# All generated adapter rows in SBUF: the first batch's rows go straight to its weight tile, the stores to DRAM follow the last chunk

## The reference

```python
dWd = ((h_lang @ Wdd.T + bdd) * DELTA_SCALE).reshape(B, BN, D)   # B 16, BN 128, D 256, h_lang 16x64
dWu = ((h_lang @ Wdu.T + bdu) * DELTA_SCALE).reshape(B, D, BN)   # Wdd, Wdu: 32768 x 64 each
Wd_b = Wd + dWd
Wu_b = Wu + dWu
down = relu(einsum('bld,bnd->bln', x, Wd_b) + bd)
up = einsum('bln,bdn->bld', down, Wu_b) + bu
x = x + up
```

## Time and profile before

| | us |
|---|---|
| median of 3 runs | 892.39 (890.39 to 892.61) |
| profiled execution, its own time | 892.63 |
| its span | 890.8 |
| PE busy | 812.6 (91%) |
| DVE busy | 551.5 (62%) |
| ACT busy | 520.9 (58%) |
| POOL busy | 234.1 (26%) |

### The profile page before, as it was taken

How to read it: one execution, slowest core, us unless ns; L and a number is a source line. 1 busy time by engine, 2 the same in 40 slices (tenths; PEclk the granted TensorE clock), 3 DMA queues, 4 the chain that set the end, 5 groups by cost and what they waited for, 6 DMA issues and landing times.

```text
span 890.8 us, 15973 instructions
## 1 busy us (share of the span) xinstructions
PE 812.6 (91%) x5852; PEld 628.5 (71%) x5852; DVE 551.5 (62%) x1063; ACT 520.9 (58%) x808; POOL 234.1 (26%) x333
## 2 busy tenths in 40 slices
PE   6752577999999999999999999999999999999976
PEld 4101446777787878787878787878787787877665
DVE  1213667686767767585858585858585767656424
ACT  1101443566676758585867667666667676765642
POOL 1002213050505142423223241505050505030310
PEclk9755677999999999999999999999999999999999
DMA  9998733334242342525241514333333333320000
GB/s 344 358 416 314 240 139 103 126 99 163 66 166 75 112 134 85 160 86 160 84 162 56 180 58 150 95 121 125 103 130 115 108 120 107 103 101 2 31 13 13
DMA packets 58477, 118.48 MB, mean 133 GB/s; under 512 B 6336, under 2 KB 15936, under 8 KB 55696
## 3 DMA queue, kind: packets, MB, share of 16 engines
q1 hardware_dynamic: 58400, 117.48, 38.8%
HBM read 82.77 MB, written 34.16 MB: 131 GB/s over the span
## 4 chain that ended last, share of the span: by engine, by line
PE 80%; issue 6%; DMA 5%; DVE 4%; POOL 3%; ACT 1%; SPq 1%; POOLq 0%; DVEq 0%; ACTq 0%
PE bank L502 31%; PE bank L708 13%; PE pair_s L663 6%; PE pair_t L502 5%; PE bank L674 3%; PE bank L755 3%; DMA hyp<-in_hyper 3%; PE pair_s L651 3%; PE pair_s L629 3%; PE bank L567 2%; PE pair_t L651 2%; PE bank L573 2%; PE bank L747 2%; PE pair_t L629 1%; PE pair_t L511 1%
## 5 line engine op out<-in xcount | busy, mean ns | idle before, releaser
L708 PE MATMUL bank<-wf,G 128*128 128x256 f32 x512 | 126.6, 391 | 0.7 <-ACT G L884 0.5
L502 PE MATMUL bank<-wup_hi,hD_hi 128*128 128x512 f32 x256 | 110.3, 431 | 4.1 <-POOL hD_lo L1334 3.2
L869 ACT ACTIVATE Pr<-pair_s 128x1024 f32<-128x1024 f32 x64 | 65.6, 1025 | 74.9 <-PE pair_s L651 74.9
L1362 POOL TENSOR_TENSOR x<-x,xcr 128x512 f32<-128x512 f32 x16 | 20.8, 1302 | 335.4 <-DVE x L1197 335.4
L708 PEld LDWEIGHTS bank<-wf,G 128*128 128x128 f32 x512 | 92.2, 189 | 21.9 <-issue 5.8
L502 PE MATMUL bank<-wup_hi,hD_lo 128*128 128x512 f32 x256 | 101.6, 397 | 0.0
L502 PE MATMUL bank<-wup_lo,hD_hi 128*128 128x512 f32 x256 | 101.6, 397 | 0.0
L1139 DVE TENSOR_REDUCE nmax<-pair_s 128x4 f32<-128x1024 f32 x64 | 78.0, 1218 | 20.3 <-PE pair_s L629 20.1
L1163 DVE STREAM_TRANSPOSE oq<-pair_s 128x512 f32<-128x512 f32 x32 | 22.9, 717 | 88.7 <-PE pair_s L663 88.7
L1139 DVE TENSOR_REDUCE nmax<-pair_t 128x4 f32<-128x1024 f32 x64 | 77.5, 1211 | 0.0
L913 ACT ACTIVATE gl<-bank,rsD 128x512 f32<-128x512 f32 x64 | 43.8, 685 | 53.0 <-PE bank L502 52.9
(11 more groups left out here) (183 smaller groups left out, 1995.5 us busy)
## 6 DMA issues: line engine op xcount, KB each, us to landing
hyp<-in_hyper SPq DMA_DIRECT2D x16, 1024.0 KB, 10.2
Qp<-qk_scratch SPq DMA_DIRECT2D x64, 256.0 KB, 5.0
Kp<-qk_scratch SPq DMA_DIRECT2D x64, 256.0 KB, 4.6
qk_scratch<-q_hi SPq DMA_DIRECT2D x16, 512.0 KB, 2.8
qk_scratch<-k_hi SPq DMA_DIRECT2D x16, 512.0 KB, 3.3
tC<-rows_scratch SPq DMA_DIRECT2D x16, 384.0 KB, 4.3
cur_scratch<-gen SPq DMA_DIRECT2D x16, 256.0 KB, 10.1
xT_t<-in_xT SPq DMA_DIRECT2D x16, 256.0 KB, 4.1
```

The costliest lines, as they stand in the source:

```text
L502: mm = pe.matmul(dst, l, r, start=first and i == 0, stop=last and i == 2)
L708: mm = pe.matmul(bank[5][:, r * D:(r + 1) * D], G[:, k, r * P:(r + 1) * P], wf2[:, k, :], start=k == 0, stop=k == FT - 1)
L869: act.activation(Pr[:, p % 4, :, :].rearrange("p a n -> p (a n)"), pair[p % 2][:, :, :].rearrange("p a n -> p (a n)"), ACT.Exp, scale=DH * ...
```

## The change

The tile `gen` becomes 32 KB per partition with a place for each of the 16 chunks, laid over the later weights `wup_hi` and `wup_lo`; `row_t` and `tb`, which lay there, move to the staging area. With a place for each chunk, ACT and DVE no longer wait for a store before they evict, and ACT, DVE and POOL no longer wait for all the stores before turn 0. The loops over chunks are unrolled. The generator weights are laid out in another order, so that one chunk yields eight whole rows of `cur` for each batch. For each chunk SP issues `first_rows(c)`, a copy of batch 0's eight rows from `gen` to `cur` inside SBUF (8 rows of 2 KB). The stores to `cur_scratch` are four DMAs of 1024 KB behind `wqkv_raw`. `wup_raw` waits for them, since it overwrites `gen`. The gather of `cur` for the later batches is one DMA of 128 rows of 2 KB.

```diff
-        gen = staged("gen", [P, 4, HALF], F32, 4 * HALF)
+        row_t = staged("row_t", [NB, 8 * D], F32, 8 * D)
+        tb = staged("tb", [NB, 8, D], F32, 8 * D)
...
+        gen = nc.alloc_sbuf_tensor_at("gen", [P, NCH, HALF], F32, offset=wup_hi_at)
...
-            def generated(i, s):
-
-                sp.wait_ge(gen_act if s % 2 == 0 else gen_dve, i * 2 + (s // 2 + 1))
-                sp.dma_start(cur_scratch[bass.ds(i * 4 + s, 1)].rearrange("o p n -> (o p) n"), gen[:, s, :]).then_inc(gen_out[s], 16)
-
-            with sp.Fori(0, NCH // 4 - 1) as i:
-                for s in range(4):
-
-                    sp.wait_ge(hyp_mm, i * 4 + (s + 1))
-                    sp.dma_start(hyp[:, s, :], hyper[:, bass.ds((i + 1) * (4 * CHC) + s * CHC, CHC)]).then_inc(hyp_in[s], 16)
-                    generated(i, s)
+            def first_rows(c):
+
+                sp.wait_ge(gen_act if c % 2 == 0 else gen_dve, c // 2 + 1)
+                sp.dma_start(cur[8 * c:8 * c + 8, :], gen[0:P:NB, c, :]).then_inc(first_in, 16)
+
+            for c in range(4, NCH):
+                sp.wait_ge(hyp_mm, c - 3)
+                sp.dma_start(hyp[:, c % 4, :], hyper[:, c * CHC:(c + 1) * CHC]).then_inc(hyp_in[c % 4], 16)
+                first_rows(c - 4)
...
             def load_weights(b):
 
-                for u in range(2):
-                    sp.dma_start(cur[64 * u:64 * u + 64, :].rearrange("p (s n) -> p s n", s=2),
-                                 cur_rows[:, :, bass.ds(b, 1), u * D:(u + 1) * D].rearrange("r s o n -> (r o) s n")).then_inc(cur_in, 16)
-                sp.dma_start(tA[:, :, :].rearrange("p a b -> p (a b)"),
-                             rows_scratch[bass.ds(b, 1), 0:2, :].rearrange("o a b -> o (a b)").to_broadcast([P, 2 * D])).then_inc(tA_in, 16)
+                sp.dma_start(cur[:, :], cur_rows[:, bass.ds(b, 1), :].rearrange("r o n -> (r o) n")).then_inc(cur_in, 16)
+                load_gates(b)
 
             load_rows(0)
-            for s in range(4):
-                generated(NCH // 4 - 1, s)
+            for c in range(NCH - 4, NCH):
+                first_rows(c)
             sp.wait_ge(rows_out, 16)
-            for s in range(4):
-                sp.wait_ge(gen_out[s], 16 * (NCH // 4))
-            load_weights(0)
+            load_gates(0)
             sp.dma_start(wqkv_raw[:, :], w_qkv).then_inc(wqkv_in, 16)
 
+            for i in range(4):
+                sp.dma_start(cur_scratch[4 * i:4 * i + 4].rearrange("c p n -> p c n"), gen[:, 4 * i:4 * i + 4, :]).then_inc(gen_out, 16)
...
             sp.dma_start(wf1_raw[:, :], w_f1).then_inc(wf1_in, 16)
+            sp.wait_ge(gen_out, 64)
             sp.dma_start(wup_raw[:, :], w_up).then_inc(wup_in, 16)
...
             def combine(b):
 
-                dve.wait_ge(cur_in, 32 * b + 32)
+                if b == 0:
+                    dve.wait_ge(first_in, 16 * NCH)
+                else:
+                    dve.wait_ge(cur_in, 16 * b)
```

More of the change, by code:

```diff
@@ L307, in cond_seq_kernel @@
         hyp_in = [sem(f"hyp_in{i}") for i in range(4)]
-        gen_out = [sem(f"gen_out{i}") for i in range(4)]
+        gen_out, first_in = sem("gen_out"), sem("first_in")
         hyp_mm, gen_act, gen_dve = sem("hyp_mm"), sem("gen_act"), sem("gen_dve")
@@ L503, in three, with generate @@
                 return mm
-            def generate(i, s):
-                pe.wait_ge(hyp_in[s], i * 16 + 16)
-                if not isinstance(i, int):
-                    pe.wait_ge(gen_act if s % 2 == 0 else gen_dve, i * 2 + (s // 2 - 1))
+            def generate(c):
+                s = c % 4
+                pe.wait_ge(hyp_in[s], c // 4 * 16 + 16)
+                if c >= 4:
+                    pe.wait_ge(gen_act if s % 2 == 0 else gen_dve, c // 2 - 1)
                 for q in range(QTS):
@@ L525, in _ @@
             mm.then_inc(pre_pe, 1)
-            generate(0, 1)
+            generate(1)
             pe.wait_ge(wc_in, 16)
@@ L546, in _ @@
             mm.then_inc(pre_pe, 1)
-            generate(0, 3)
-            with pe.Fori(1, NCH // 4) as i:
-                for s in range(4):
-                    generate(i, s)
+            generate(3)
+            for c in range(4, NCH):
+                generate(c)
             pe.wait_ge(prep, len(PREP))
@@ L776, in _, with generated @@
         def _(act):
-            def generated(i, s):
-                if not isinstance(i, int):
-                    act.wait_ge(gen_out[s], i * 16)
-                act.wait_ge(hyp_mm, i * 4 + (s + 1))
-                act.activation(gen[:, s, :], bank[s][:, :], ACT.Copy).then_inc(gen_act, 1)
+            def generated(c):
+                act.wait_ge(hyp_mm, c + 1)
+                act.activation(gen[:, c, :], bank[c % 4][:, :], ACT.Copy).then_inc(gen_act, 1)
             act.wait_ge(prep, PREP.index("z1") + 1)
             act.activation(zb[:, 1], zb[:, 0], ACT.Exp, scale=-1.0).then_inc(pre_act, 1)
-            generated(0, 0)
+            generated(0)
             act.wait_ge(prep, PREP.index("z2") + 1)
             act.activation(zb[:, 3], zb[:, 2], ACT.Exp, scale=-1.0).then_inc(pre_act, 1)
-            generated(0, 2)
+            generated(2)
             act.wait_ge(prep, PREP.index("tbl") + 1)
@@ L796, in high_part @@
                 act.activation(hi[:, :, :].rearrange("p k n -> p (k n)"), raw[:, :], ACT.Copy).then_inc(act_w, 1)
-            with act.Fori(1, NCH // 4) as i:
-                for s in (0, 2):
-                    generated(i, s)
+            for c in range(4, NCH, 2):
+                generated(c)
             act.wait_ge(rows_out, 16)
             act.wait_ge(prep, len(PREP))
-            for s in range(4):
-                act.wait_ge(gen_out[s], 16 * (NCH // 4))
             def qkv_weights():
@@ L975, in after_last, with generated @@
                 dve.wait_ge(prep, done[0])
-            def generated(i, s):
-                if not isinstance(i, int):
-                    dve.wait_ge(gen_out[s], i * 16)
-                dve.wait_ge(hyp_mm, i * 4 + (s + 1))
-                dve.tensor_copy(gen[:, s, :], bank[s][:, :]).then_inc(gen_dve, 1)
+            def generated(c):
+                dve.wait_ge(hyp_mm, c + 1)
+                dve.tensor_copy(gen[:, c, :], bank[c % 4][:, :]).then_inc(gen_dve, 1)
             mm4 = bank[4][:, 0:KT * NB].rearrange("p (k n) -> p k n", k=KT)
@@ L1031, in _ @@
             assert done[0] == len(PREP)
-            with dve.Fori(1, NCH // 4) as i:
-                for s in (1, 3):
-                    generated(i, s)
+            for c in range(5, NCH, 2):
+                generated(c)
             def low_part(hi, lo, raw, step_):
@@ L1047, in _ @@
             dve.wait_ge(rows_out, 16)
-            for s in range(4):
-                dve.wait_ge(gen_out[s], 16 * (NCH // 4))
             def combine(b):
-                dve.wait_ge(cur_in, 32 * b + 32)
+                if b == 0:
+                    dve.wait_ge(first_in, 16 * NCH)
+                else:
+                    dve.wait_ge(cur_in, 16 * b)
                 dve.wait_ge(dve_w, at(DVE_W, "base", 0))
@@ L1292, in _ @@
             pool.wait_ge(rows_out, 16)
-            for s in range(4):
-                pool.wait_ge(gen_out[s], 16 * (NCH // 4))
             pool.wait_ge(zero, 7)
@@ L1436 @@
         "x": c(x.reshape(NB, RT, P, D).transpose(0, 2, 1, 3)),
[L1437 to L1439 removed]
+        "hyper": c(np.concatenate([by_part(arr(L0_cond_Wdd).T), arr(L0_cond_Wdu).T.reshape(HC, D, BN).transpose(0, 2, 1)], 2)
+                   .reshape(HC, P // 2, 2, 2 * D).transpose(2, 0, 1, 3).reshape(2 * HC, -1)),
         "base": c(np.concatenate([by_part(wd)[0], wu.T, by_part(bdd)[0], bdu.T], 1)),
```

19 lines of the change are left out of this document (8 added, 11 removed).

## The result

| | median of 14 runs, us | profiled span |
|---|---|---|
| before | 891.42 (889.59 to 892.61) | 890.8 |
| changed | 894.53 (892.71 to 897.61) | 892.6 |

The ratio over all runs is 1.0047, with a 95% interval of 1.0036 to 1.0057; the two medians alone stand 3.1 us or 0.35% apart. 889.9 was forecast (884.5 to 893.8), and the measured time lies outside the range. The head start is there, and more than all of it is gone before the second turn.

The account below looks back on a forecast made before the run. It took the front as bound by the 16 DMA engines and PE as full from the eighth slice on. 5.5 (generation) + 5.8 (tail) - 8.8 (turn 0 waiting) = 2.5 us gained: 889.9, range 884.5 to 893.8.

Parts of the forecast that it names:

- head start: Start of turn 0: `combine(0)` at 61.2 us instead of 72.52, so turn 0 starts 11.3 us earlier.
- The deciding row: DVE's second `cur<-cur,base_c`: expected near 93 us after waiting 16 us or more; at 96 the kernel is no faster.
- The ledger of the queue: DMA queue before batch 1's loads: `wqkv_raw` at 66.0 to 66.4 us, 10.4 of stores, everything behind 0 to 0.6 later.
- the other branch: PE in turn 0: `a_down(1)` starts with `xT_t` at 94.3 us, and DVE's `x` gains 2.8 us.
- the forecast landing: Batch 1's gather of `cur`: within a few tenths of its present landing, with 93.1 us taken for DVE.
- the forecast gain: Whole kernel: DVE's first maximum of turn 1 starts 2.5 us earlier, and this is carried to the end.
- The generation term: Chunk loop: 2.47 us a chunk without stores among the loads, so chunk 15 lands 5.5 us earlier, at 56.0.
- The tail's 5.8: Behind the last chunk: one 16 KB copy, taken as 2.3 us, replaces store and gather; 5.8 us saved.
- The third term, -8.8: Turn 0 waiting for the queue that now holds the stores: 8.8 us lost.
- the queue's idle gap: DMA queue from behind the last store (67.6 us) to the gather's issue: claimed to be moved by the change, not filled.
- the debt that outweighs the head start: Rival at DVE's `A.cur` of batch 1: kernel slower, 893.5 to 897 us; chance 0.12.
- the three conditions: For a slower kernel: reads below 386 GB/s, stores over 12.5 us, or the queue running dry during SP's wait.

## Why the prediction was wrong

**What it had right.** PE's full middle: what happens at the front arrives at the end as a shift. The deciding row, DVE's second `cur`. The ledger of the queue: it had 37.1 us from the last matmul's start (56.0) to `combine(1)` (93.1); measured are 95.45 - 57.79 = 37.7. The wait on `gen_out` without effect of its own (402, 392 and 430 GB/s in the three steps of 2 us from 76), SP reaching the gather ahead of the time of before, the lower level of the clock in `a_down(1)`.

**The step that failed.** "On the other branch `a_down(1)` starts with `xT_t` at 94.3 instead of 98.99". It doesn't: PE runs in program order, and `a_v` stands in front of it with the line `pe.wait_ge(dve_a, at(DVE_A, "qlo1", a))`, since v is accumulated in the bank from which `q_lo` reads. So the branch was not another one but the same chain: gather, `combine(1)`, `q_lo`, v, `Va`, `a_down`, `a_up`. The prediction had PE done with v "before 88" by shifting the whole of PE's turn by 11.3 us, without asking for each row which engine it waits for, although it had just found that `q_lo` would not shift. It thus had 1.2 us from `combine(1)` to `a_down(1)` (93.1 to 94.3) where 5.24 were measured (95.45 to 100.69): 0.6 to `q_lo`, 0.9 to v, 2.97 to `Va`, 0.7 to `a_down`. From `a_down(1)` to `x` it had 4.7, the lower level of the clock counted in, and 4.73 were measured. So of the 6.4 us by which `x` is later than forecast (105.42 against 99.0), 4.0 are the links of the chain that it left out, and 2.4 the later landing. 1.4 of the 4.0 are the lower level of the clock in v, which it did not have either. The kernel with `cur` behind k removes just this wait and gets some 3 us back. Even at the forecast landing most of the forecast gain would have been missing: with `combine(1)` at 93.38 and 93.72, `x` was at 101.45 and 103.69, where 99.0 was forecast and the kernel before has 101.83.

**The mis-sized term.** "Copies to `cur` are 16 KB each, 12 of them in the loop: 0.2 MB, nothing." They are nothing in bytes, and the loop ran at 407 GB/s instead of 424. The generation term of 5.5 us measured 61.55 - 57.79 = 3.8. That is one execution against one: the eight kernels with this loop have the last matmul at 56.23 to 58.25, so only the 0.2 us a chunk is sure of this 1.7. The tail's 5.8 measured (72.52 - 61.55) - (62.55 - 57.79) = 6.2, since the last copy lands in 1.85 us rather than 2.3. Together 10.0 instead of 11.3. The third term, -8.8, measured -13.6: `x` of batch 1 is 3.6 us late. By the medians the end is 3.1 late.

**The term that was right in size and wrong in meaning.** The stores have 10.4 us in the sum, and at the 406 GB/s of 66 to 78 us their 4.19 MB take 10.3. But the prediction wrote of the queue's idle gap that it "is not filled by the change but moved". The gap, and the loop before it, is where the stores belonged: the kernel with the stores in the loop has moved 2.3 MB more by its end, and is 6.2 us faster than the changed one and 0.4% faster than before (ratio 0.9964). The change is thus two, of opposite sign: the direct copy for batch 0 with the dropped waits, worth some 3 us, and the deferral of the stores, which costs 6.

**The rivals.** It went the way of the debt that outweighs the head start, at the place that this rival names, with 894.5 in its interval of 893.5 to 897; it had a chance of 0.12. That its interval was hit is luck. Of the three conditions that it names none came: the loads ran at 407 GB/s, not under 386, the stores took 10.3 us, not over 12.5, and the queue did not run dry. Its price was too low, for the same reason as above: by its rule (it decides from a landing at 95, and each further us costs one) a landing at 95.4 would have cost 0.4 us and not 3.1.

**The rule weighed.** The Trainium skill (DMA: Bandwidth & Descriptors, Where 436 GB/s comes from) has the HBM side bind at about 358 GB/s. The changed kernel loads at 407 GB/s and the one without copies at 421, so this trace does not bear it out; for the loads that came slower than forecast the kernel without copies shows another reason.
